# Four-bit up weights prepared at the end of the latent attention, and a projection fed by halves of its context

## The reference

```python
# latent attention (16 heads of 16; half of each head's q and k is rotated by position)
kv_d, q_d = x @ W_kvD.T, x @ W_qD.T
k = cat(kv_d @ W_kU.T, rope(x @ W_rk.T));  q = cat(q_d @ W_qU.T, rope(q_d @ W_rq.T))
probs = softmax(causal(q @ k.T * scale));  attn = probs @ (kv_d @ W_vU.T)
x = layernorm(x + attn @ W_o.T)

# four-bit layer (H = 1024 hidden, blocks of 64 weights share a scale, low-rank additions of rank 16)
w_up = ((w_up_q - 7.5) * repeat(w_up_scale, 64)).T
x2 = relu(x @ w_up + b_up + x @ w_up_lora_a @ w_up_lora_b)
w_down = ((w_down_q - 7.5) * repeat(w_down_scale, 64)).T
x = layernorm(x + x2 @ w_down + b_down + x2 @ w_down_lora_a @ w_down_lora_b)
```

## Time and profile before

| | |
|---|---|
| median of 3 runs | 1679.51 us (1677.98 to 1684.59) |
| the profiled execution's own time | 1675.68 us |
| its span | 1673.7 us |
| busy: PE, PEld, DVE | 1535.9, 1272.2, 1054.1 us |
| busy: ACT, POOL | 872.8, 490.9 us |
| mean granted clock of TensorE | 0.97 |

### The profile page before, as it was taken

The page is one execution under the profiler, slowest core; times in us unless marked ns, Lnnn a source line. Parts: engine busy times, 40 slices in busy tenths (PEclk is TensorE's granted clock), DMA queues, the critical chain, the costliest instruction groups (busy, mean ns, idle before and its releaser), DMA issues. The chain is left out here.

```text
span 1673.7 us, 27839 instructions
## 1 busy us (share of the span) xinstructions
PE 1535.9 (92%) x9791; PEld 1272.2 (76%) x9791; DVE 1054.1 (63%) x2017; ACT 872.8 (52%) x1954; POOL 490.9 (29%) x563
## 2 busy tenths in 40 slices
PE   7899979999999999997798879889999999997987
PEld 6678868788779788886466556778888888876955
DVE  2665446566565544444577741678888888887965
ACT  3343336565565433333466634466666666665634
POOL 0045535254242065553833122110111111102300
PEclk9899999999999899999899979999999999998999
DMA  5221110000001463310345230100000000001000
GB/s 125 78 94 51 51 51 20 19 0 19 0 1 39 128 157 92 100 51 0 60 57 63 26 78 1 55 20 20 10 9 19 19 9 9 19 1 53 2 1 26
DMA packets 76099, 68.23 MB, mean 41 GB/s; under 512 B 32176, under 2 KB 67208, under 8 KB 76016
## 3 DMA queue, kind: packets, MB, share of 16 engines
q1 hardware_dynamic: 71312, 62.73, 14.2%
q0 software_dynamic: 4704, 4.40, 2.2%
HBM read 56.46 MB, written 1.21 MB: 34 GB/s over the span
## 5 line engine op out<-in xcount | busy, mean ns | idle before, releaser
L2496 ACT ACTIVATE diff_att_probs<-psum,diff_att_neg_max 128x512 f32<-128x512 f32 x256 | 174.6, 696 | 28.0 <-DVE diff_att_neg_max L2560 28.0
L2560 DVE TENSOR_REDUCE diff_att_neg_max<-psum 128x2 f32<-128x1024 f32 x128 | 153.1, 1217 | 26.4 <-PE psum L2386 26.3
L1371 POOL TENSOR_TENSOR gqa_att_probs<-gqa_att_probs,gqa_att_inv_sum 128x128 f32<-128x128 f32 (+3 forms) x128 | 88.3, 723 | 159.9 <-DVE gqa_att_inv_sum L1505 159.9
L2407 PE MATMUL psum<-x_feat,diff_att_mixed_t 128*128 128x128 f32 x1024 | 126.0, 277 | 0.9 <-ACT diff_att_mixed_t L2502 0.8
L2407 PEld LDWEIGHTS psum<-x_feat,diff_att_mixed_t 128*128 128x128 f32 x1024 | 122.8, 193 | 4.4 <-issue 1.9
L495 POOL TENSOR_TENSOR ahead_w_hi<-ahead_w,ahead_zeros 128x512 fp32r<-128x512 f32 x16 | 16.7, 1041 | 276.4 <-DMA ahead_w<-in_L_attn_Wv 276.3
L1466 ACT ACTIVATE gqa_att_probs<-psum,gqa_att_neg_max 128x128 f32<-128x128 f32 (+3 forms) x128 | 66.6, 526 | 55.2 <-DVE gqa_att_neg_max L1499 55.2
L989 POOL TENSOR_TENSOR top_scaled<-top_scaled,top_wb 128x512 f32<-128x512 f32 x48 | 66.6, 1394 | 86.3 <-DVE top_scaled L967 81.1
L2572 DVE SCALAR_TENSOR_TENSOR diff_att_mixed<-diff_att_probs,diff_att_ratio 128x512 f32<-128x512 f32 x128 | 87.7, 747 | 1.1
L1778 POOL DMA_DIRECT2D mla_att_q_own<-mla_att_parts x144 | 71.1, 503 | 57.3 <-PE psum L1863 52.9
L967 DVE TENSOR_TENSOR top_scaled<-top_gate,psum 128x512 f32<-128x512 f32 x48 | 32.9, 686 | 78.2 <-PE psum L101 56.7
(11 more groups left out here) (517 smaller groups left out, 4910.3 us busy)
## 6 DMA issues: line engine op xcount, KB each, us to landing
top_wb<-top_w_dram SPq DMA_DIRECT2D x16, 384.0 KB, 4.0
golden_wb<-golden_w_dram SPq DMA_DIRECT2D x8, 512.0 KB, 4.7
top_wb<-top_w_dram SPq DMA_DIRECT2D x16, 256.0 KB, 4.2
mla_att_k_feat<-mla_att_parts SPq DMA_DIRECT2D x56, 64.0 KB, 4.9
mla_att_q_own<-mla_att_parts POOLq DMA_DIRECT2D x112, 32.0 KB, 3.8
ahead_w_nat<-in_L_ffn_w SPq DMA_DIRECT2D x16, 192.0 KB, 3.0
ahead_w_nat<-in_L_ffn_v SPq DMA_DIRECT2D x16, 192.0 KB, 4.3
top_down_w<-in_L_ffn_w SPq DMA_DIRECT2D x1, 3072.0 KB, 11.7
```

Of the source, the lines that this page charges most:

```text
L1371: last = nc.gpsimd.tensor_tensor(tile, tile, inv_sum[:, s, qt:qt + 1].to_broadcast([P, (qt + 1) * P]), ALU.mult)
L2407: last = nc.tensor.matmul(bank[6][:, qt * P:(qt + 1) * P], mixed_t[:, u % 2, kt, qt * P:(qt + 1) * P], v_tok[:, head, b * QT + kt, :], sta ...
L2496: last = nc.scalar.activation(probs[:, qt, m, :], bank[2 * (qt % 2) + m], ACT.Exp, bias=neg_max[:, qt, m:m + 1], accum_out=row_sum[:, qt, ...
L2560: nc.vector.tensor_reduce(neg_max[:, qt, :], psum[:, 2 * (qt % 2):2 * (qt % 2) + 2, :], AX.X, ALU.max, negate=True).then_inc(maxed, 1)
```

## The change

It has five parts.

1. Pair 1 of the attention's heads is staged otherwise: k by halves of the tokens, and of q the first head's 8 transfers are issued by ACT, after its copies of unit 0, instead of by POOL. Units 4, 5 and 6 wait each for what they read.
2. SP loads the four-bit up weights, scales and small matrices after it has staged pair 2. They go where nothing is in use: the integers to `x_feat`, `up_b` to a table tile of the attention; `inv` shares another one.
3. After its last copy of the attention ACT centres the up weights in place and copies wo's high part (into `x_lo`); POOL scales the weights and makes wo's low part. PE, after the last pair's product, transposes the small matrices and builds two of the four quarters of the up weights in banks 0 and 1.
4. In the four-bit layer the context is split by halves of the tokens, and the first half of the projection waits for its own half only. Filler products and the waits for wo and the scales are gone. `up_b` is loaded again.
5. ACT reads the two built quarters before the layer norm's roots, and DVE splits them between the moments and the normalising. The other two quarters are built right after the projection, no longer between hidden jobs.

```diff
@@ class Closing @@
+        if self.between:
+            self.between(dve)
...
@@ class LatentContext(Prefetch) @@
+    SHAPES = {"ctx": ([P, DC, T], F32), "wo_t": ([P, DC, D], F32), "up_scale": ([P, HC, D // BLOCK], F32), "up_a": ([P, DC, R], F32),
+              "down_a": ([P, HC, R], F32), "b_rows": ([HC, P], F32), "up_at": ([R, D], F32), "b_up": ([P, HC], F32)}
...
+    def load(self, sp, up_b):
+        t, W = self.t, lambda n: self.env.src[f"L2_ffn_{n}"]
+        sp.dma_start(self.up_q().rearrange("p (c d) -> p c d", d=D), W("w_up_q").rearrange("(c p) d -> p c d", p=P)).then_inc(self.sem["up_loaded"], 16)
+        sp.dma_start(t["up_scale"][:], W("w_up_scale").rearrange("(c p) k -> p c k", p=P)).then_inc(self.sem["up_loaded"], 16)
+        for dst, dram in ((t["up_a"][:], W("w_up_lora_a").rearrange("(c p) r -> p c r", p=P)), (up_b, W("w_up_lora_b")),
+                          (t["down_a"][:], W("w_down_lora_a").rearrange("(c p) r -> p c r", p=P)),
+                          (t["b_rows"][:], W("b_up").rearrange("(c p) -> c p", p=P))):
+            sp.dma_start(dst, dram).then_inc(self.sem["small_loaded"], 16)
+
+    def scalar(self, act):
+        t, sem = self.t, self.sem
+        act.wait_ge(sem["up_loaded"], 32)
+        self.nc.scalar.activation(self.up_nat(), self.up_q(), ACT.Copy, bias=-7.5).then_inc(sem["centred"], 1)
+        act.wait_ge(sem["centred"], 1)
+        self.nc.scalar.activation(self.wo_part(0), t["wo_t"][:], ACT.Copy).then_inc(sem["wo_high"], 1)
+        bank = self.env.bank
+        act.wait_ge(sem["at_made"], 1)
+        self.nc.scalar.activation(t["up_at"][:], bank[4][0:self.R, 0:D], ACT.Copy).then_inc(sem["at_read"], 1)
+        self.nc.scalar.activation(t["b_up"][:], bank[4][:, D:D + self.HC], ACT.Copy)
+
+    def gpsimd(self, pool):
...
+        self.nc.gpsimd.tensor_tensor(whole, whole, scale, ALU.mult).then_inc(sem["dequantised"], 1)
+        pool.wait_ge(sem["wo_high"], 1)
+        self.nc.gpsimd.tensor_tensor(self.wo_part(1), t["wo_t"][:], self.wo_part(0).bitcast(F32), ALU.subtract).then_inc(sem["wo_split"], 1)
...
+    def tensor(self, pe, up_b):
+        nc, bank, ident, t, sem = self.nc, self.env.bank, self.env.ident, self.t, self.sem
+        pe.wait_ge(sem["small_loaded"], 64)
+        for c in range(DC):
+            nc.tensor.transpose(bank[4][0:self.R, c * P:(c + 1) * P], t["up_a"][:, c, :], ident[:])
+        nc.tensor.transpose(bank[4][:, D:D + self.HC], t["b_rows"][:], ident[0:self.HC, 0:self.HC]).then_inc(sem["at_made"], 1)
+        pe.wait_ge(sem["at_read"], 1)
+        pe.wait_ge(sem["dequantised"], 1)
+        for j in range(2):
+            self.up_part(j, up_b).then_inc(sem["up_made"], 1)
@@ latent_attention @@
-                stage_k(sp, 1, slice(0, T), staged[1])
+                    stage_k(sp, 1, half_cols(half), second_staged if half == 0 else staged[1])
                 for p in range(2, PAIRS):
                     sp.wait_ge(scores_made, (p - 1) * PUNITS * QT)
                     stage_k(sp, p, slice(0, T), staged[p % 2])
+                    if p == 2:
+                        nxt.load(sp, up_b)
...
-                    if n == PAIR or n % PUNITS == 0 and p:
+                    if n == PUNITS:
+                        pe.wait_ge(second_staged, STAGED)
+                        pe.wait_ge(second_q_staged, STAGED)
+                    elif n == PUNITS + 1:
+                        pe.wait_ge(staged[1], STAGED)
+                    elif n == PUNITS + 2:
+                        pe.wait_ge(q_staged[1], STAGED)
...
                 attend(PAIRS - 1, UNITS)
+                nxt.tensor(pe, up_b)
...
-                stage_q(pool, 1, 0, slice(0, T), q_staged[1])
                 stage_q(pool, 1, 1, slice(0, T), q_staged[1])
...
+                pool.wait_ge(w_read_dve, 2)
+                nxt.gpsimd(pool)
...
+                    if n == 0:
+                        act.wait_ge(zeroed, 2)
+                        act.wait_ge(nope_low, 4)
+                        act.wait_ge(rope_low, 4)
+                        stage_q(act, 1, 0, slice(0, T), second_q_staged)
+                act.wait_ge(w_read_dve, 2)
+                nxt.scalar(act)
@@ four_bit_ffn, PE @@
-                keep_busy(nc, env, bank[0], 9)
-                for c in range(DC):
-                    pe.wait_ge(ctx_split, c + 1)
-                    pe.wait_ge(wo_split, c + 1)
+                for c in range(HC):
+                    last = nc.tensor.transpose(bank[2 + c // 4][0:R, (c % 4) * P:(c % 4 + 1) * P], down_a[:, c, :], ident[:])
+                last.then_inc(at_made, 1)
                 for t in range(NT):
+                    if t % 4 == 0:
+                        pe.wait_ge(ctx_split, t // 2 + 2)
...
-                pe.wait_ge(at_read, 4)
-                pe.wait_ge(dequantised, 1)
-                up_part(0)
-                up_part(1)
+                pe.wait_ge(at_read, 2)
+                pe.wait_ge(up_b_loaded, 16)
+                for j in (2, 3):
+                    pre.up_part(j, up_b[:]).then_inc(w_made, 1)
                 close.tensor(pe, waiting=False)
...
-                    if j == UP_SECOND:
-                        up_part(2)
-                        up_part(3)
@@ four_bit_ffn, ACT @@
-                for c in range(DC):
-                    nc.scalar.activation(ctx_hi[:, c], ctx[:, c], ACT.Copy).then_inc(ctx_high, 1)
-                    nc.scalar.activation(wo_hi[:, c], wo_t[:, c], ACT.Copy).then_inc(wo_high, 1)
-                act.wait_ge(up_loaded, 32)
-                nc.scalar.activation(flat(up_nat), flat(up_q), ACT.Copy, bias=-7.5).then_inc(centred, 1)
+                for half, c, cols in ctx_cols:
+                    nc.scalar.activation(ctx_hi[:, c, cols], ctx[:, c, cols], ACT.Copy).then_inc(ctx_high, 1)
...
-                close.scalar(act)
                 read_up(0)
                 read_up(1)
+                close.scalar(act)
+                read_up(2)
+                read_up(3)
```

More of the change, by code:

```diff
@@ L193, in scalar @@
                     act.wait_ge(self.feat_copied, half + 1)
-                for c in range(DC):
+                for c in range(DC) if self.parts else ():
                     if not self.whole:
@@ new lines, in up_part @@
+    def up_part(self, j, up_b):
+        c, hh = j % 2, j // 2
+        nc, bank, ident, nat = self.nc, self.env.bank, self.env.ident, self.up_nat().rearrange("p (c d) -> p c d", d=D)
+        nc.tensor.matmul(bank[j], self.t["up_at"][:, c * P:(c + 1) * P], up_b[:, hh * 512:(hh + 1) * 512], start=True, stop=False)
+        for i in range(4):
+            last = nc.tensor.matmul(bank[j][:, i * P:(i + 1) * P], nat[:, 4 * hh + i, c * P:(c + 1) * P], ident[:], start=False, stop=i == 3)
+        return last
@@ L2086, in four_bit_ffn, with first_up_lows @@
+            def first_up_lows(dve):
+                up_low(dve, 0)
+                up_low(dve, 1)
+            close = Closing(nc, env, "fin4", up, None, False, acc, lambda eng, t: eng.wait_ge(projected, t // 2 + 1), first_bank=4,
+                            between=first_up_lows)
             block = up.block()
             flat = lambda a: a[:].rearrange("p c d -> p (c d)")
-            up_parts = [(0, 0), (1, 0), (0, 1), (1, 1)]
+            ctx_cols = [(half, c, slice(half * HALF, (half + 1) * HALF)) for half in range(2) for c in range(DC)]
```

122 lines of the change are left out of this document (53 added, 69 removed).

## The result

The changed kernel took 1664.92 us, the median of five runs (1662.15 to 1667.28), against 1678.49 for the kernel before (five runs, 1677.05 to 1684.59): a ratio of 0.9917, with a 95% interval of 0.9901 to 0.9934, 0.8% faster. The forecast was 1666.4, in a range of 1660 to 1673. Its total held, but its terms were off, and the errors cancelled: one step lost 4.5 us where 1.3 was expected, and the other stretches gave between 0.2 and 1.2 us more than expected. So the match of the total is in part luck.

A forecast was written before the change was run, and what follows sets the result against it. The prediction took both stages to be chains of waits. Its terms, 3.5 - 1.0 - 1.3 + 11.9 = 13.1 us, took the profiled 1675.68 to 1662.6; with 3.8 carried for the median, 1666.4 us, range 1660 to 1673.

The forecast's parts named there:

- Part 1: Staging of pair 1 of the attention's heads: unit 4's scores start at 832.5 instead of 836.05, 3.5 us gained.
- ACT's price of an issue: In pair 1's staging, each of ACT's eight q transfers takes 0.84 us to issue, the mean of SyncE's issues then.
- the 2 us that were named as a sign of being wrong: In pair 1's staging, ACT's issues above 2 us would show the forecast wrong.
- The wait of about 4 us before unit 4: In the attention, PE's wait before unit 4 shrinking to about 4 us would show the forecast right.
- The rival on the other side: In pair 1's staging, ACT is held 4.34 us by each issue and every exponential waits: 1694.3 us, chance 6%.
- Part 2: Six loads on SyncE's queue inside the attention, between pair 2's and pair 3's k, can delay pair 3: 1.0 us lost.
- Its cover of 1.0 us: In the attention, pair 3's last k lands at the latest at 870.1, 1.0 us before unit 12 uses it.
- its upper end: For the six loads inside the attention, a loss of up to 5 us, with issues of 2.9 us ending 6 late.
- The second rival: The loads hold up pair 3 in the attention, k coming 6 us late: 1671.4 to 1673 us, chance 12%.
- Part 3: End of the attention: PE's two up quarters end behind DVE's last multiply, GpSimd's scaling hidden by PE's last product: 1.3 us lost.
- Part 4: Four-bit layer: earlier projection 1.5 us, shorter chain to the hidden layer 6.3, quarters leaving the hidden products 4.1; 11.9 gained.
- The third rival: Half clock under both pairs of up quarters, at the attention's end and in the four-bit layer: 1672.2 us, chance 7%.

The follow-up runs named there:

- e1: The changed kernel with GpSimd's two late instructions (scaling the up weights, low part of the output weights) moved to DVE: 1660.41 us, 0.989 of the kernel before.
- e5: The kernel before, with one 128x1 memset added on GpSimd behind the attention's last product: 1685.39 us against 1679.19, a ratio of 1.0042.
- e6: The changed kernel with all of GpSimd's q transfers issued by SyncE, GpSimd keeping its two late instructions: 1684.22 us, one run.
- e8: The changed kernel with e3's staging and the up weights prepared earlier, one quarter ahead of the attention's last product: 1654.4 us, 0.9853 of the kernel before.
- e9: The changed kernel with its first two up quarters built in the four-bit layer behind the projection: 1673.25 us, 0.9962 of the kernel before.
- e2: The changed kernel with pair 1 of the heads staged as before the change: 1670.48 us, 0.9947 of the kernel before.
- e3: The changed kernel with GpSimd issuing all of pair 1's q, first head first on its own semaphore, ACT none: 1663.91 us, 0.992 of the kernel before.
- e10: The changed kernel with the projection waiting for all four splits of the context before its first product: 1668.14 us, 0.994 of the kernel before.
- e7: The changed kernel with the edits of e1 and e3 together: 1660.75 us, 0.9892 of the kernel before.

## Why the total was right and its terms were not

**What closes the block.** One rule fits all twelve kernels, of which seven are shown: the block opens 0.9 us behind the latest of three ends.

| us | PE's last product | DVE's last multiply | GpSimd's drain | block opens |
|---|---|---|---|---|
| before | 967.76 | 972.68 | 942.75 | 973.58 |
| changed | 972.59 | 971.31 | 975.88 | 976.76 |
| e1 | 973.18 | 971.66 | 940.25 | 974.09 |
| e5 | 970.57 | 975.49 | 981.25 | 982.13 |
| e6 | 996.42 | 995.12 | 989.56 | 997.33 |
| e8 | 963.50 | 966.29 | 936.87 | 967.19 |
| e9 | 962.29 | 966.74 | 971.86 | 972.73 |

**Part 1** (3.5 forecast). e2 puts it at 2.5 us in the trace, 5.6 in the medians. The size is about right and the step to it wrong. The term that was off is ACT's price of an issue: 0.84 forecast, 1.13 measured, 0.63 to 2.45 apiece, so that one issue passed the 2 us that were named as a sign of being wrong; and behind the issues stood 4.6 us (832.96 to 837.54) where 3.5 were counted. So unit 4 itself gained only 0.4. The wait of about 4 us before unit 4 that was to show the forecast right isn't there: PE waits 6.61 us, before unit 3. The gain came from that shorter wait and from less time at half clock behind it, neither of which the forecast had looked at; that it came near 3.5 is luck. The rival on the other side, ACT held for 4.34 us an issue, was wrong in size, not in kind: ACT's issues were the bound, and e3 shows unit 4 5.7 us earlier without them.

**Part 2** (1.0 lost). It cost nothing. Unit 12 had no wait, though the loads did hold pair 3 up: SyncE's six issues ran from 850.28 to 856.44, and pair 3's first k followed at 856.49. From the view of the changed kernel's k transfers, the eight of pair 3:

```profile
L1841 SPq DMA_DIRECT2D mla_att_k_feat<-mla_att_parts x8: 525/951/3563, 856.5 to 866.0; - x8
...
DMA to landing us min/median/max: 2.5/4.1/6.9
```

Counted from the first scores, the first and the last issue both came 1.8 us later than before. But the last landed 2.5 behind its issue, at 868.5: 1.7 us ahead of unit 12. Two steps of the forecast were off. Its cover of 1.0 us took the longest landing, 7.8, for the last transfer's; that one had landed after 6.5, so the cover was 2.3. And its upper end doesn't follow from its own numbers: six issues of 2.9 from 844 end at 861.4, 12 us behind 849 and not 6. The second rival's time rests on that 6; measured, the six issues took 6.2 us together.

**Part 3** (1.3 lost). The step about PE and DVE came out (1.28; 1.52 in e1), though 1.3 was a choice between 0.2 and 4.3, so that its nearness is in part luck. What failed is the sentence that costed GpSimd's scaling at nothing because PE's last product hides its 3.63 us: the instruction was hidden, the drain behind it was not. It lost 4.55 us, and 3.0 of that come back when another engine does the work (e1's stretch is 2.43, of which 1.5 are PE's quarters). The drain of before, 14.59 us at 928.2, was there to be read; the forecast had looked only at busy time.

**Part 4** (11.9). 13.8 measured; by e10's trace it is 14.4. The projection starts 3.84 us behind the opening instead of 5.37, so the 1.5 came out, but nothing of it is the halves' (e10). It is left to the missing fillers, which before the change ran until the projection's first product at 978.95, and to wo's low part, which POOL had ready only at 978.2 and which is now made in the stage before; no run parts the two. The chain to the hidden layer ends with x_lo, as forecast, and gave 7.0 for 6.3; with e10's 15.0 us for the changed kernel's 13.9 it would be 5.8, so the 0.7 are within the scatter. Of the 5.3 us behind that, the quarters between the hidden products gave 4.0 if both stretches are multiplied by their clock (42.41 x 0.89 against 37.11 x 0.91), and less half clock the rest.

The third rival, half clock under the quarters, was right in part: of the two quarters at the attention's end the second needed 2.08 us for its eight products with the identity, the first 1.16; those behind the projection needed 1.16 each and so ran at full clock. The other signs that the prediction had named came true: no wait before units 8 and 12, and the first hidden product 16.7 us behind the block's first product (977.75).

## What to carry to other kernels

Work moved to the end of a block on an idle engine also moves that engine's closing drain; look for the drain's own row, and if GpSimd has issued transfers in the block, give it nothing late (e5: a memset of 0.10 us cost 6). Before adding an issuer, split the waits, so that the first consumer waits only for what it needs (e3). And prepare next-stage data where the trace shows idle time, not where the old stage ends (e8).

## What was not expected of the hardware

GpSimd's drain ended 10.2 to 10.5 us behind its last instruction in the block where it issues transfers (the changed kernel, e5, e9), and 0.1 us behind it where it issues none (e6). ACT, which in the changed kernel issued eight transfers in that block, had no such drain: its own took 0.45 us, from 966.9 on.

GpSimd's issue kept its 0.50 us (497 to 511 ns in e3) while SyncE, in the same 13 us, took up to 3.71 and ACT, in the changed kernel, up to 2.45. The Trainium skill (DMA: Bandwidth & Descriptors, SWDGE vs HWDGE vs iDMA) calls the path of SyncE and ACT the one with the faster setup; with small transfers close together the rows here show the opposite for the time that an issue takes its engine.

The spread of the runs goes with the clock: the five runs of the changed kernel took 1662.15, 1663.43, 1664.92, 1665.72 and 1667.28 us at mean granted clocks of 0.974, 0.973, 0.972, 0.971 and 0.970. One stretch of code, the hidden layer, took 34.0 us at full clock (e1, e7) and 37.1 to 37.2 at 0.91 (the changed kernel, e8). What the traces do show is that it goes with PE's idle time between the two blocks. In the three in which PE stood idle for 1.90 us there (e1, e6, e7) the hidden layer was granted full clock throughout; in the other nine, in which it stood idle for 4.69 us (e8) to 12.55 us (e5), 5.17 in the changed kernel, it was granted 0.84 to 0.97. If the one is the other's cause, the late drain cost the changed kernel the hidden layer's 3.1 us as well as its own 3.0. But that is one execution of each kernel, and no run changes the idle time alone, so the cause stays open.
